# Expanding q for all four columns of a step in one run on TensorE, ahead of the spread of the next scores

## The reference, cut to what matters

```python
h = jnp.maximum(_layernorm(x), 0.0)
q, k, v = linear(h, wq, bq), linear(h, wk, bk), linear(h, wv, bv)
scores = jnp.sum(q[dst] * k[src], axis=-1) * scale
scores = scores + (edge_weight[:, None] @ we + be)[:, 0]
seg_max = jax.ops.segment_max(scores, dst, num_segments=n)
exp_s = jnp.exp(scores - seg_max[dst])
denom = jax.ops.segment_sum(exp_s, dst, num_segments=n)
attn = exp_s / jnp.maximum(denom[dst], 1e-12)
out = jax.ops.segment_sum(v[src] * attn[:, None], dst, num_segments=n)
x = layer_norm(h + out + linear(h, ws, bs), g1, b1)
x = layer_norm(x + ffn(x), g2, b2)
```

## Time and profile before

| | |
|---|---|
| median of 3 runs | 2336.25 us |
| lowest and highest run | 2335.91 and 2336.41 us |
| span of the profiled execution, first to last instruction | 3211.3 us |
| time of the profiled execution around its span | not recorded |
| busy in the profile: TensorE, its weight loads | 2427.3 us (76%), 1996.1 us (62%) |
| VectorE, ScalarE, GpSimd | 1767.6 (55%), 1193.2 (37%), 1635.5 us (51%) |
| mean granted TensorE clock in the profile | 0.921 of 2.4 GHz |

### The profile page before, as it was taken

How to read it: one execution, slowest core, us unless ns; L and a number is a source line. 1 busy time by engine, 2 the same in 40 slices (tenths; PEclk the granted TensorE clock), 3 DMA queues, 4 the chain that set the end, 5 groups by cost and what they waited for, 6 DMA issues and landing times. The chain is left out here.

```text
span 3211.3 us, 68474 instructions
## 1 busy us (share of the span) xinstructions
PE 2427.3 (76%) x14747; PEld 1996.1 (62%) x14748; DVE 1767.6 (55%) x7372; ACT 1193.2 (37%) x2930; POOL 1635.5 (51%) x1828
## 2 busy tenths in 40 slices
PE   7577677777777777777777777777777777778998
PEld 5455556556555556565656566665666666657897
DVE  7454455555555545554555555555555555556787
ACT  6333333333333333333333333333333333334666
POOL 5355565555555545555554555555555445441154
PEclk8898899899899989998998999899988899999999
DMA  7233333333233323333233333332333233222222
GB/s 231 76 103 103 99 105 101 103 98 107 90 100 100 96 86 101 97 98 96 90 102 92 96 90 96 96 98 87 96 96 100 87 92 95 83 93 71 82 74 68
DMA packets 148148, 311.29 MB, mean 97 GB/s; under 512 B 33566, under 2 KB 84625, under 8 KB 148104
## 3 DMA queue, kind: packets, MB, share of 16 engines
q0 software_dynamic: 75264, 205.62, 21.5%
q1 hardware_dynamic: 54718, 90.19, 8.6%
q10 hardware_dynamic: 18122, 14.96, 1.5%
HBM read 290.21 MB, written 20.43 MB: 97 GB/s over the span
## 5 line engine op out<-in xcount | busy, mean ns | idle before, releaser
L488 POOL DMA_INDIRECT work<-h_rows,idx x1536 | 1457.3, 949 | 1339.9 <-SPq L372 956.2
L1079 PE MATMUL bank<-work 128*128 x3520 | 939.0, 412 | 24.5 <-issue 17.7
L1011 PE MATMUL bank<-q,onehot 128*128 x5304 | 804.6, 291 | 1.2 <-DVE work L832 0.7
L1079 PEld LDWEIGHTS bank<-work 128*128 128x128 f32 x3520 | 700.1, 211 | 146.8 <-issue 45.2
L886 DVE CUSTOM_DVE_ANT_0 work<-bank,work 128x512 f32<-128x512 f32 x440 | 330.5, 751 | 778.7 <-remote 476.4
L622 ACT COPY work<-bank 128x256 f32<-128x256 f32 x880 | 295.0, 376 | 1182.6 <-remote 812.8
L832 DVE SCALAR_TENSOR_TENSOR work<-bank,work 128x257 bf16<-128x257 f32 x1764 | 651.6, 425 | 143.5 <-PE bank L1011 44.2
L1017 PE MATMUL bank<-ident,work 128*128 128x128 f32 x1764 | 307.4, 302 | 500.5 <-ACT work L622 313.3
L1011 PEld LDWEIGHTS bank<-q,onehot 128*128 128x128 bf16 x5304 | 549.5, 104 | 85.4 <-issue 1.7
L1017 PEld LDWEIGHTS bank<-ident,work 128*128 128x128 f32 x1764 | 212.8, 148 | 578.0 <-ACT work L622 442.4
L1066 PE MATMUL bank<-ident,work 128*128 128x128 f32 x1760 | 283.6, 285 | 191.8 <-ACT work L619 182.8
(11 more groups left out here) (195 smaller groups left out, 1519.5 us busy)
## 6 DMA issues: line engine op xcount, KB each, us to landing
dst_words<-dst_short SPq DMA_DIRECT2D x99, 512.0 KB
work<-h_rows,idx POOLq DMA_INDIRECT x1568
bias<-h_rows ACTq DMA_DIRECT2D x56, 128.0 KB
r_rows<-bias ACTq DMA_DIRECT2D x55, 128.0 KB
work<-r_rows SPq DMA_DIRECT2D x49, 128.0 KB, 2.3
h_rows<-acc SPq DMA_DIRECT2D x12, 512.0 KB, 6.6
work<-in_x SPq DMA_DIRECT2D x12, 512.0 KB, 3.5
out<-work SPq DMA_DIRECT2D x48, 128.0 KB, 1.7
```

Of the source, the lines that this page charges most:

```text
L488: pool.indirect_dma_start(rows[:, u, j, 0:D], None, h_rows, bass.IndirectOffsetOnAxis(idx[:, half, u * J + j:u * J + j + 1], 0)).then_inc( ...
L1011: last = nc.tensor.matmul(banks[j][:, 0:D1], onehot[:, k, j, :], q3[:, bass.ds(b, 1), c, 0:D1], start=(c == 0), stop=(c == 2))
L1079: last = nc.tensor.matmul(banks[6 + k][:, 0:D1], probs[:, j, :], rows[:, bass.ds(slot, 1), j, :], start=(j == 2), stop=(j == 1))
```

## The change

In the edge loop TensorE expanded the first half of q for step s + 2, then waited for the scores and the probabilities' first copy and spread the scores of step s + 1, and then expanded the second half. Now both halves are expanded ahead of these waits and of the spread. Each half keeps its wait for the dots that read its banks. `expand_q` signals `q_edges` after the second half alone, once per step, and VectorE waits for it once before its four dots.

A second edit goes with it. Values loaded into registers get a mask (`not_below_zero`), an added register operation that keeps the bits up to the highest possible value: in the counts at the start of each engine's loop, in VectorE's step numbers, and in SP's slot numbers.

```diff
...
         spread, max_read, masked_done, max_kept = (sem(n) for n in ("spread", "max_read", "masked_done", "max_kept"))
         exp_done, turned, probs_done, summed, added = (sem(n) for n in ("exp_done", "turned", "probs_done", "summed", "added"))
+        def not_below_zero(eng, loaded, min_val, max_val):
+
+            mask = (1 << max_val.bit_length()) - 1
+            return eng.snap(eng.to_reg(eng.snap(loaded) & mask), min_val=min_val, max_val=max_val)
+
         def counts(eng):
             regs = [eng.alloc_register(n) for n in ("trips", "last_trips", "rounds")]
             eng.load(regs, n_trips[0:1, 0:3])
-            n = eng.snap(regs[0], min_val=NW, max_val=TRIPS)
+            n = not_below_zero(eng, regs[0], NW, TRIPS)
             m = eng.snap(regs[1], min_val=0, max_val=1)
-            return n, m, eng.snap(regs[2], min_val=1, max_val=B)
+            return n, m, not_below_zero(eng, regs[2], 1, B)
         def trips(eng, body):
...
                                 sp.wait_ge(dst_out, 2 * 16)
                                 sp.wait_ge(rows_in[u][j], landed)
                             sp.sem_inc(chunk_landed, 1)
-                            used_up = sp.to_reg(sp.snap(regs[u], min_val=1, max_val=T + B + S) + r * TP)
+                            used_up = sp.to_reg(not_below_zero(sp, regs[u], 1, T + B + S) + r * TP)
                             sp.wait_ge(dst_out, 2 * 16)
                             sp.wait_ge(summed, used_up)
                             sp.sem_inc(slot_free, 1)
                             if u % WC == 0:
                                 window = trip * 2 + (u // WC + 1)
-                                before, marks = sp.to_reg(window * 16), sp.to_reg(sp.snap(regs[u + WC - 1], min_val=1, max_val=T + B + S) + r * TP)
+                                before, marks = sp.to_reg(window * 16), sp.to_reg(not_below_zero(sp, regs[u + WC - 1], 1, T + B + S) + r * TP)
                                 half = (u // WC + 1) % 2 * WC * C
                                 sp.wait_ge(dst_out, 2 * 16)
                                 sp.wait_ge(dst_in, before)
...
                 sp.wait_ge(dst_in, last)
                 all_turns = sp.alloc_register("all_turns")
                 sp.load(all_turns, n_trips[0:1, 3:4])
-                all_back = sp.to_reg(sp.snap(all_turns, min_val=NW, max_val=B * NW) * 16 + 16)
+                all_back = sp.to_reg(not_below_zero(sp, all_turns, NW, B * NW) * 16 + 16)
                 sp.wait_ge(late_in, 7 * 16)
-                sp.wait_ge(r_copied, sp.to_reg(sp.snap(all_turns, min_val=NW, max_val=B * NW) + 1))
+                sp.wait_ge(r_copied, sp.to_reg(not_below_zero(sp, all_turns, NW, B * NW) + 1))
                 sp.dma_start(wv_sb[:], wv.rearrange("(c p) n -> p c n", p=P)).then_inc(out_in, 16)
                 sp.wait_ge(late_in, 7 * 16)
                 sp.wait_ge(h_back, all_back)
...
                     dve.wait_ge(plan_done, 1)
                     nc.vector.memset(banks[7][:, 0:D1], 0.0).then_inc(sums_set, 1)
                     dve.load(regs[0:3], steps_tab[0:1, 0:3])
-                    ahead[:] = [dve.snap(v, min_val=0, max_val=TP * BLOCKS) for v in regs[0:3]]
+                    ahead[:] = [not_below_zero(dve, v, 0, TP * BLOCKS) for v in regs[0:3]]
                     blocks[:] = [block_of(dve, v) for v in ahead]
                     dve.sem_inc(added, 1)
                     dve.sem_inc(max_kept, 1)
...
                     chunk = chunk_of(dve, step)
                     slot = slot_of(dve, chunk)
                     column = dve.snap(dve.to_reg((chunk - r * TP) * J), min_val=0, max_val=R)
-                    there, first_half, second_half = dve.to_reg(chunk + 1), dve.to_reg(s * 2 + 1), dve.to_reg(s * 2 + 2)
+                    there, expanded, second_half = dve.to_reg(chunk + 1), dve.to_reg(s + 1), dve.to_reg(s * 2 + 2)
                     dve.wait_ge(chunk_landed, there)
-                    for half, ready in ((0, first_half), (1, second_half)):
-                        dve.wait_ge(q_edges, ready)
+                    dve.wait_ge(q_edges, expanded)
+                    for half in range(2):
                         for j in (2 * half, 2 * half + 1):
                             last = nc.vector.scalar_tensor_tensor(out=product[:, j, 0:D1], in0=banks[j][:, 0:D1], scalar=SCALE, in1=rows[:, bass.ds(slot, 1), j, :],
                                                                   op0=ALU.mult, op1=ALU.mult, accum_out=dots[:, k, j:j + 1])
...
                     blocks = {}
                     def step_at(v):
-                        return dve.snap(v, min_val=0, max_val=(TP + U + HALF) * BLOCKS) + r * ROUND
+                        return not_below_zero(dve, v, 0, (TP + U + HALF) * BLOCKS) + r * ROUND
                     def block_at(u):
                         if u not in blocks:
...
                     for j in (2 * half, 2 * half + 1):
                         for c in range(3):
                             last = nc.tensor.matmul(banks[j][:, 0:D1], onehot[:, k, j, :], q3[:, bass.ds(b, 1), c, 0:D1], start=(c == 0), stop=(c == 2))
-                    last.then_inc(q_edges, 1)
+                    if half == 1:
+                        last.then_inc(q_edges, 1)
                 def spread_scores(k):
...
                         pe.wait_ge(onehot_done, s + (S + 3))
                         pe.wait_ge(dotted, s * 2 + 3)
                         expand_q(k, 0, b)
+                        pe.wait_ge(dotted, s * 2 + 4)
+                        expand_q(k, 1, b)
                         pe.wait_ge(scored, s + 2)
                         pe.wait_ge(probs_done, s * 2 + 1)
                         spread_scores(1 - k)
-                        pe.wait_ge(dotted, s * 2 + 4)
-                        expand_q(k, 1, b)
                         for j in (2, 3, 0, 1):
                             if j == 0:
                                 pe.wait_ge(probs_done, s * 2 + 2)
```

## The result

The changed kernel takes **2656.06 us** (median of four runs, 2655.19 to 2663.16), the kernel before 2336.08 in the same call: a ratio of 1.138, with a 95% interval of 1.136 to 1.140. The forecast was 2379 us, range 2334 to 2458. The sign was right, the size was not: 277 us are missing from it.

The account below looks back on a forecast made before the run. Gathers pace most of the edge loop, steps its last quarter. At 4.37 us a step its stretches sum to 1001 + 489 + 496 = 1986 us against 1943, +43: 2336.25 + 43 = 2379 us, range 2334 to 2458.

Parts of the forecast that it names:

- "I take 0" for the masks: VectorE's added register instructions, bounded at 0 to 0.38 us a step, stay under the 4.31 us step and cost 0.
- The move: Second expansion ahead of the spread in TensorE's edge loop: 4.37 us a step against 4.09, +43 us in all.
- Chain 3.64 + 0.67 = 4.31: Path from one spread to the next, 3.64 us, gains the second expansion's 0.67 and exceeds TensorE's own 3.94.
- TensorE's idle time 0.53: Between spread and turns TensorE has 2.06 us of work for a 2.59 us chain, so it idles 0.53 us.
- "Gathers pace most of the loop, the steps its last quarter": GpSimd's gathers, one every 1.25 us, set most of the edge loop before the change: 1943 us against 1930 in the runs.
- the same three stretches: Edge loop split into 214, 112 and 113.5 steps, each taking the longer of its gathers and its steps.
- A: Steps pace the whole edge loop before and after; +123 us, 2459 us; chance 0.17.
- B: No effect: the edge loop's path is 0.3 us a step shorter in the runs, the second expansion fits; 2336 us; chance 0.12.
- C: Faster: sum and slot release come 0.67 us sooner, shortening the ring of eight slots; -32 us, 2304 us; chance 0.08.
- D: TensorE's clock falls in the new pauses, in a tenth of the steps; 55 us on top of 43, 2434 us; chance 0.05.
- The cover of the moved spread: The spread's wait behind the last two dots costs 0, with 0.46 us of cover before the second expansion is due.

Follow-up runs that it names:

- e15: e2 with 94 one-column memsets on VectorE ahead of its loop; 2347.57 us, ratio to the kernel before 1.004 to 1.008.
- e13: The changed kernel with 94 one-column memsets on VectorE ahead of its loop; 2385.01 us, ratio to the kernel before 1.020 to 1.023.
- e3: The changed kernel (new order, one signal) with 16-bit tables and no masks; 2516.31 us, ratio to the kernel before 1.076 to 1.079.
- e2: The changed kernel with its old order and two signals back, masks kept; 2536.28 us, ratio to the kernel before 1.084 to 1.088.
- e11: e5 with three gathers a chunk in place of four; 2255.81 us, ratio to the kernel before 0.964 to 0.967.
- e12: e6 with three gathers a chunk in place of four; 2372.98 us, ratio to the kernel before 1.014 to 1.017.
- e6: The changed kernel with VectorE's step numbers masked once at their load, not at each use; 2395.70 us, ratio to the kernel before 1.025 to 1.028.
- e5: Old order, two signals, 32-bit tables, VectorE's step numbers masked once at their load; 2343.80 us, ratio to the kernel before 1.003 to 1.006.
- e7: The changed kernel with 62 one-column memsets on VectorE ahead of its loop; 2616.90 us, ratio to the kernel before 1.119 to 1.123.
- e8: The changed kernel with 30 one-column memsets on VectorE ahead of its loop; 2618.59 us, ratio to the kernel before 1.120 to 1.124.
- e9: e6 with 20 more register instructions a trip in VectorE's loop body; 2686.89 us, ratio to the kernel before 1.148 to 1.152.
- e10: e6 with 40 more register instructions a trip in VectorE's loop body; 2649.65 us, ratio to the kernel before 1.133 to 1.137.

## Why the prediction was wrong, point by point

**The failed step: "I take 0" for the masks.** The prediction costed them as work, two register operations a step beside VectorE's slack, and bounded them at 57 us. The count was short (38 more instructions a trip are 4.75 a step), but as work they were cheap: e15, all masks in the old order at a fitting place, is 13.7 us above the kernel before. What it never costed is their code. Between the branch of a trip's end and VectorE's next instruction lie 3.65 us at the median in the changed kernel and 0.29 in e13; the trip's last step takes 8.99 us for 5.12. The pause then brings a second cost: after 4.39 us without a matmul TensorE was granted 0.61 of 2.4 GHz in the window above (a mix of its levels 1.2 and 2.4), and the first step takes 6.04 for 4.38. Each of the 54 pauses at a trip's end in the changed kernel was followed by a stretch at 1.2 GHz. e3, without fetches but with pauses of some 2 us, prices the clock apart: its first step took 4.99 us in the 33 trips with 1.00 granted and 6.22 in the 22 with less. Together (3.87 + 1.66) x 55 = 304 us, against 271 measured between the kernels (2656.06 - 2385.01); the other steps give a little back, since in e13 gathers still lengthen some. Without the move the masks cost 200 us, by e2 and e15 nearly all of it through the fetching (2536.28 - 2347.57 = 189).

**The move: right.** Chain 3.64 + 0.67 = 4.31 was forecast, 4.32 is there; TensorE's idle time 0.53, there 0.55. The trip was forecast to grow by 34.9 - 32.7 = 2.2 us; with gathers out of the way it grew from 34.2 to 36.3 (e11, e12). The price of the move was forecast at 43 us and is 37 (e13 - e15) to 52 us (e6 - e5). Had the code fitted, the answer would have been 2385 for a forecast 2379.

**"Gathers pace most of the loop, the steps its last quarter": right**, though inferred from a stretched profile (the register instruction that took up to 700 ns in the earlier trace rows takes 45 ns at its shortest, median and longest in the profile after). Two terms were off and cancelled: the first stage takes 115 us, not 143, and a trip ends with a load of the step numbers and a branch, so that it takes 34.2 us, not 32.7 (its last step is 5.5 us for 3.94). Put into the same three stretches, 4.27 us a step gives 914, 478 and 485, and the longer ones 1001 + 478 + 485 = 1964 us; e5's loop is 1961 (114.9 to 2076.2). Steps alone give 914 + 478 + 485 = 1877, 87 less, and e11 fell by 88. The new order, 4.54 a step, gives 1001 + 508 + 515 = 2024; e6's is 2017.

**The rivals.** A (steps pace the whole loop, +123) is what happens in the changed kernel as it is, though not for A's reason: the fetching makes trips so long that the gathers no longer cover anything, and the move costs its full 120 us (2656.06 - 2536.28). The two edits' costs therefore do not add: at a fitting place the move costs 37 to 52 us, beside the fetching 120. B and C did not occur. In D, the 0.5 us pauses did not touch the clock, 1.00 in the clean window above; the Trainium skill's warning of short pauses ("TensorE: Matmul & The Clock Gate", section "A second HAM failure mode: psum-queue depth-cycling") is not borne out by them. The clock fell after the pauses of over 4 us at the trip's end, which D did not have, and after some of the 2 us pauses of e3.

**The cover of the moved spread** held, as forecast: the dots never came last, and in the waits of TensorE the dots (L837) stand with one wait of 1.4 us, ahead of the expansion (L1016) and not of the spread.

Left open: why one fetch is longer than another. From the branch to VectorE's next instruction it is 3.89 us in the mean in the changed kernel and 3.20 and 3.21 in e7 and e8, which over 54 trips is the 38 us that 62 or 30 instructions ahead took off; between e9 (3.66) and e10 (3.18) it is 26 of 37 us. That the kernel before stays within its pieces is by its count and its 24 packets. No version here that computes the same beats it; e5 and e15 come within 0.6%.

## What to carry to other kernels

An instruction in an unrolled loop has two prices, its time and its place: count the loop body of each engine, and read the packets of the instruction queue on the page. If they grow with the trips, look at the branch, and move the loop by idle instructions ahead of it, by several amounts, before anything else is judged (here 30 and 62 did not help and 94 did). And when two resources pace stretches in turn, an edit's cost depends on the other's slack, so it has to be measured in the state that will stay.

## What the runs showed of the hardware that was not expected

- Whether the code of VectorE's loop is fetched anew in each trip depends on where the body lies and not only on its length. In the changed kernel it was: about five packets of 8.2 KB a trip (271 more in 54 trips), 3.4 us at the branch, and with what follows 271 us. Moving the same code by 94 instructions removed all of it; moving a body of 291 by 30 brought it (241 us).
- A pause of 4.80 us in TensorE's loads was followed by a granted clock of 0.61 over the next 3.8 us, where twelve loads took 2.09 us for 1.32; all 54 pauses of this kind were followed by such a stretch. Pauses of 0.55 us a step left the clock at 1.00.
- Loading the registers of a trip from a table of 16-bit words took 2.92 us, from 32-bit words 0.85.
- GpSimd's gathers of 128 rows, back to back, start 1.251 to 1.254 us apart at the median in every kernel here, as in the earlier trace rows.
